# Rows of the expert slots turned by transposing loads from 16-bit planes, and four products of a kind in a row

## The reference

```
xn = layernorm(x)
y  = x + attention(xn) + ffn(xn)

attention: q = xn Wq^T + bq (16 heads of 16), k, v = one shared head of 16 each
           strictly causal softmax(q k^T / 4) v, then Wo, bo
ffn:       scores = sigmoid(xn w_router); 32 experts in 8 groups; 4 groups, then 6 experts are picked per token
           routed = sum over the picked e of score_e * (silu(xn gate_e) * (xn up_e)) down_e      (M = 176)
           shared = (silu(xn sh_gate) * (xn sh_up)) sh_down                                       (352 wide)
```

## Time and profile before

| | us |
|---|---|
| median of 3 runs | 644.38 |
| lowest, highest | 642.62, 650.23 |
| the profiled execution's span | 648.6 |
| PE busy in it | 579.2 (89%) |
| POOL, DVE, ACT busy | 324.4, 350.6, 277.4 |

### The profile page before, as it was taken

How to read it: one execution, slowest core, us unless ns; L and a number is a source line. 1 busy time by engine, 2 the same in 40 slices (tenths; PEclk the granted TensorE clock), 3 DMA queues, 4 the chain that set the end, 5 groups by cost and what they waited for, 6 DMA issues and landing times.

```text
span 648.6 us, 12417 instructions
## 1 busy us (share of the span) xinstructions
PE 579.2 (89%) x4250; PEld 331.8 (51%) x4250; DVE 350.6 (54%) x921; ACT 277.4 (43%) x537; POOL 324.4 (50%) x265
## 2 busy tenths in 40 slices
PE   4998887888999899999799999999999999999900
PEld 2444333444555455464456566665656566565700
DVE  6637684894675566211355555546455554546136
ACT  2755223344543443546445454554545354454200
POOL 5122330320466755775046566666767676767600
PEclk9999998998999899999999999999999999999965
DMA  8697988699699963699346665566565655666598
GB/s 304 182 170 104 376 322 275 47 351 368 191 299 347 362 201 119 191 338 368 123 100 106 114 126 91 96 108 130 88 125 89 121 94 117 110 108 95 63 334 325
DMA packets 72555, 122.84 MB, mean 189 GB/s; under 512 B 10864, under 2 KB 56112, under 8 KB 71984
## 3 DMA queue, kind: packets, MB, share of 16 engines
q1 hardware_dynamic: 47808, 85.02, 43.8%
q0 software_dynamic: 20736, 29.05, 24.2%
q10 hardware_dynamic: 3952, 8.00, 3.5%
HBM read 61.41 MB, written 62.52 MB: 191 GB/s over the span
## 4 chain that ended last, share of the span: by engine, by line
PE 45%; POOL 15%; issue 14%; DMA 13%; DVE 8%; ACT 3%; SPq 1%; ACTq 0%; DVEq 0%; POOLq 0%
POOL acc_d L1319 13%; PE bank L1553 8%; PE bank L1583 5%; DMA acc_d<-attT,xnT 5%; PE bank L1423 5%; PE bank L1405 5%; PE bank L1379 4%; DVE mx L948 3%; PE bank L1494 3%; DMA k_d<-weights 2%; PE bank L1486 2%; PE bank L1352 2%; PE bank L1407 2%; DMA weights<-mpart 2%; PE bank L1382 2%
## 5 line engine op out<-in xcount | busy, mean ns | idle before, releaser
L1319 POOL DMA_INDIRECT acc_d<-attT,xnT x112 | 192.6, 1720 | 122.2 <-DMA acc_d<-attT,xnT 73.6
L1553 PE MATMUL bank<-weights,xnT 128*64 x448 | 143.4, 462 | 1.8 <-DVE attT L1101 1.7
L1276 POOL DMA_INDIRECT xg_d<-stage,posu x96 | 92.5, 963 | 75.4 <-issue 55.1
L948 DVE TENSOR_REDUCE mx<-bank 128x1 f32<-128x384 f32 (+7 forms) x154 | 105.1, 708 | 43.3 <-PE bank L1382 40.9
L766 ACT ACTIVATE xnT<-bank 128x1024 f32<-128x1024 f32 (+1 forms) x72 | 62.0, 884 | 81.0 <-PE bank L1407 76.4
L1553 PEld LDWEIGHTS bank<-weights,xnT 128*64 128x64 f32 x448 | 58.7, 136 | 63.0 <-issue 51.4
L827 ACT ACTIVATE attT<-bank,xnT 128x256 f32<-128x256 f32 x112 | 46.9, 470 | 83.1 <-PE bank L1586 83.1
L1556 PE MATMUL bank<-attT,xnT 128*64 128x352 f32 x224 | 76.9, 466 | 0.0
L1556 PE MATMUL bank<-shared_sb,xnT 128*64 128x352 f32 x224 | 75.5, 459 | 0.0
L812 ACT ACTIVATE xnT<-bank 128x176 f32<-128x176 f32 x112 | 35.5, 317 | 72.9 <-PE bank L1556 72.9
L1101 DVE COPY attT<-weights 128x704 f32 x56 | 29.5, 527 | 48.9 <-PE bank L1556 41.2
(11 more groups left out here) (161 smaller groups left out, 1094.8 us busy)
## 6 DMA issues: line engine op xcount, KB each, us to landing
weights<-in_wts SPq DMA_DIRECT2D x32, 608.0 KB
xg_d<-weights SPq DMA_DIRECT2D x28, 584.0 KB, 9.5
stage<-xg_d SPq DMA_DIRECT2D x14, 584.0 KB, 4.1
xnT<-xg_d SPq DMA_DIRECT2D x14, 584.0 KB
acc_d<-weights SPq DMA_DIRECT2D x8, 512.0 KB, 10.2
q_d<-weights SPq DMA_DIRECT2D x8, 384.0 KB, 5.5
weights<-q_d SPq DMA_DIRECT2D x12, 256.0 KB, 8.8
weights<-q_d SPq DMA_DIRECT2D x48, 64.0 KB, 6.6
```

Of the source, the lines that this page charges most:

```text
L948: eng.tensor_reduce(mx[:, b % 2, h0:h0 + nh * pair, i].rearrange("p (k h) -> p k h", k=pair), bank[:, k:k + pair, 0:wide].rearrange("p k ( ...
L1276: eng.indirect_dma_start(out=xg_d[:, :], out_offset=bass.IndirectOffsetOnAxis(ap=posu[:, t, k:k + 1], axis=0), in_=stage[:, t % NST, :], i ...
L1319: eng.indirect_dma_start(out=acc_d[a][:, :], out_offset=bass.IndirectOffsetOnAxis(ap=index[:, i // RS % NIX, i % RS:i % RS + 1], axis=0), ...
L1553: eng.matmul(bank[0:SR, k, 0:2 * M], rows[:, c, 0:SR], weights[:, bass.ds(expert[i] * WCOL + c * 2 * M, 2 * M)], start=(c == 0), stop=(c = ...
```

## The change

- Rows are kept in DRAM in another form. POOL splits each normalized row of 256 float32 into two planes of 16-bit words (`part_planes`): first the low halves of all columns, then the high halves. Eight copies, two tiles each, into `planes`, which holds four tiles. `rows(g)` stores `planes` in place of `xn`, all eight on SP. `normalize` of tiles 8 to 15 waits for `part_planes` in place of the store.
- The rows of a round come from DRAM by a transposing load (`load_turned`) of 512 rows by 512 16-bit columns into `rows16` (one buffer, in the place of `stage`), and the 36 last words of each row by a load of their own (`load_tails`, two buffers, 144 bytes a row).
- DVE copies the low halves (`merge_low`) and ACT the high halves (`merge_high`) of four slots into `xgT`, each second 16-bit word, which makes float32 of them again. `pair_turn` and `pair_turned` are gone.
- In a round PE does the four gate/up products, then the four down products of the round before. "sb" has the four banks 0 to 3 in place of 2 and 3.
- The views for the slot stage move, so that only columns 1024 to 2047 of `xnT` hold them beside `xgT`.

```diff
+            def load_turned(j):
+                if j == 0:
+                    for n in range(NST):
+                        w.wait_ge(sent[n], 16 * TOPK * NT // NST)
+                for done in merged_half if j else ():
+                    w.wait_ge(done, j)
+                eng.dma_start_transpose(rows16, xg_d16[RS * j * P:RS * (j + 1) * P, 0:2 * D]).then_inc(turned_in, 16)
+
+            def load_tails(j):
+                if j == 1:
+                    k, n = used["down", B - 2, IT - 1]
+                    w.wait_ge(filled[k], n)
+                if j >= 2:
                     w.wait_ge(weight_done, j - 1)
...
-                    load_rows(0)
+                    load_turned(0)
+                    load_tails(0)
+            load_turned(1)
             for j in range(1, ROUNDS):
-                load_rows(j)
+                load_tails(j)
+                if j + 1 < ROUNDS:
+                    load_turned(j + 1)
...
+            def merge_high(j):
+                w.wait_ge(turned_in, 16 * (j + 1))
+                w.wait_ge(pv_done, nth["PV", B - 1, NG - 1, 1])
+                if j >= 2:
+                    k, n = used["sb", RS * (j - 1) - 1]
+                    w.wait_ge(filled[k], n)
+                eng.copy(halves[j % 2][:, :, :, 1], rows16[:, KC:, :]).then_inc(merged_half[1], 1)
...
             for j in range(ROUNDS + 1):
-                for n in range(2):
-                    for i in slots_of(j, n) if j else ():
-                        if i + 2 < NSLOT:
-                            second_gate_up(i + 2)
-                        slot_gated(i)
-                    for i in slots_of(j - 1, 1) if n == 0 else ():
-                        second_down(i)
+                for n, i in enumerate(slots_of(j)) if j else ():
+                    if i + 2 < NSLOT:
+                        second_gate_up(i + 2)
+                    slot_gated(i)
+                    if n == 1 and j + 1 < ROUNDS:
+                        merge_low(j + 1)
+                if j == 0:
+                    merge_low(1)
+                for i in slots_of(j - 1)[2:] if j else ():
+                    second_down(i)
                 if j < ROUNDS:
                     round_weights(j)
-                for i in slots_of(j, 0):
+                for i in slots_of(j)[0:2]:
                     second_down(i)
...
+            def part_planes(g):
+                w.wait_ge(norm_done, 2 * g + 2)
+                if g >= 2:
+                    w.wait_ge(row_out[(g - 2) % 4], 16 * ((g - 2) // 4 + 1))
+                s, s4 = 2 * g % NXN, 2 * g % 4
+                eng.tensor_copy(planes[:, s4:s4 + 2, :].bitcast(U16).rearrange("p t (h d) -> p t h d", h=2),
+                                xn[:, s:s + 2, :].bitcast(U16).rearrange("p t (d h) -> p t h d", h=2)).then_inc(planes_done, 1)
...
-                k2, n2 = used["sa", i // 2]
-                w.wait_ge(emptied[k2], n2)
+                for done in merged_half:
+                    w.wait_ge(done, i // RS + 1)
                 w.wait_ge(second_gu_done, i + 1)
-                rows = xgT[i // 2 % 2][:, i % 2]
+                rows = xgT[i // RS % 2][:, :, i % RS * P:(i % RS + 1) * P]
...
             for j in range(ROUNDS + 1):
-                for n in range(2):
-                    for i in slots_of(j, n) if j else ():
-                        slot_gate_up(i)
-                    for i in slots_of(j - 1, n):
-                        slot_down(i)
-                for p in pairs_of(j + 1):
-                    pair_turn(p)
+                for i in slots_of(j) if j else ():
+                    slot_gate_up(i)
+                for i in slots_of(j - 1):
+                    slot_down(i)
                 for p in pairs_of(j):
                     pair_turn_hidden(p)
```

More of the change, by code:

```diff
@@ L46 @@
 ROW = TOKEN + 4
+TAIL = ROW - D
+PLANES = 2 * D // P
 HUGE = 3e38
@@ L256, in make_plan @@
     steps += attend_steps(streams)
-    steps += [("sa", 0), ("heads", B - 1, NG - 1), ("sa", 1), *[("sb", i) for i in range(RS)],
-              ("attT", B - 1, 0), ("attT", B - 1, 1)]
+    steps += [("begin",), ("heads", B - 1, NG - 1), *[("sb", i) for i in range(RS)], ("attT", B - 1, 0), ("attT", B - 1, 1)]
     plan = Plan()
@@ L364, in build @@
         lrec = sbv("lrec", [P, 2, IT, ST_GROUP])
+        planes = carve([4, D])
         q32 = carve([NPB, T])
@@ L618, in load @@
                     w.wait_ge(comb_out, 16)
+                    for i in range(4):
+                        w.wait_ge(row_out[i], 32)
                     w.wait_ge(init_in, 16 * INITS)
@@ L1081, in round_weights, with merge_low @@
                 own.mark(eng.tensor_tensor(weight[:, j % NIX, :, 0:E], weight[:, j % NIX, :, 0:E],
-                                           xg[j % 2][:, :, D:TOKEN], ALU.mult))
+                                           tails[j % 2][:, :, 0:E], ALU.mult))
                 w.wait_ge(dve_step, own.n)
                 eng.tensor_reduce(weight[:, j % NIX, :, E], weight[:, j % NIX, :, 0:E], AX, ALU.add).then_inc(weight_done, 1)
+            def merge_low(j):
+                w.wait_ge(turned_in, 16 * (j + 1))
+                w.wait_ge(pv_done, nth["PV", B - 1, NG - 1, 1])
+                if j >= 2:
+                    k, n = used["sb", RS * (j - 1) - 1]
+                    w.wait_ge(filled[k], n)
+                eng.tensor_copy(halves[j % 2][:, :, :, 0], rows16[:, 0:KC, :]).then_inc(merged_half[0], 1)
             second = {}
@@ L1163, in vector_program @@
                     with_bias(*a)
-                elif kind == "sa" and a[0] < 2:
-                    second_gate_up(*a)
+                elif kind == "begin":
+                    second_gate_up(0)
+                    merge_low(0)
+                    second_gate_up(1)
                 elif kind == "sb":
@@ L1287, in gpsimd_program @@
                         deviations(*a)
+                elif kind == "rows":
+                    part_planes(*a)
                 elif kind == "proj2" and sub_by[tuple(a)] == "pool":
@@ L1523, in last_down @@
                 ins.then_inc(filled[k], 1)
-            def pair_turn(p):
-                k, n = used["sa", p]
-                for k2, n2 in before["sa", p]:
-                    w.wait_ge(emptied[k2], n2)
-                j = p // 2
-                w.wait_ge(gathered[j % 2], 16 * (j // 2 + 1))
-                for m in range(2):
-                    for c in range(KC):
-                        ins = eng.transpose(bank[:, k, (KC * m + c) * P:(KC * m + c + 1) * P],
-                                            xg[j % 2][:, 2 * p % RS + m, c * P:(c + 1) * P], id_sb)
-                ins.then_inc(filled[k], 1)
             expert = {}
```

126 lines of the change are left out of this document (53 added, 73 removed).

## The result

The kernel after took 661.44 us (median of four runs, 654.69 to 666.49), the kernel before on the same chip 645.11 (642.62 to 650.23): a ratio of 1.019, 95% interval 1.012 to 1.026. (Ratios compare only executions in the faster of two states that the times fall into, so they are not the quotients of the medians, here 1.025.) I had forecast 627. The profiled execution was 660.4 us long by its span, 11.8 more than before. The medians differ by 16.3: the profiled execution of before was the longest of its four (650.23), and where the other 4.5 us lie the profiles don't show.

The account below looks back on a forecast made before the run. PE's rounds (10.24 us) and POOL's add chain (10.49) were taken to bound the kernel. 28 rounds save 20.7 us, early terms add 3.1: 644.4 - 17.6 = 627; own range 612 to 638, reaching 690 for 8 in 10.

Parts of the forecast that it names:

- The planes on POOL: Early part: eight part_planes copies at 1.2 us each, with waits for row stores, add 2 us.
- a rival of 11 us: Early part: planes copies at 2.36 us and slow stores cost 11 us instead of 2, so 636; no chance given.
- My own sign of being wrong: Attention start: prediction is wrong if PE's first row-max matmul comes more than 4 us later than now.
- The start: Start of the slots: PE waits for merge_low(0) between the first two gate-weight copies, +1.1 us.
- The transposing load: Rounds' row load: lands in 6 us, between bounds of 4.1 and 11.2, hidden below about 8 us.
- The merges: DVE's merge_low 1.1 us, its cover just used up (0.1 or 0.2 us); ACT's merge 1.02 us, with room.
- PE's own round: Slot rounds on PE: without the turning matmuls, 0.93 us a round, 10.24 us becomes 9.31.
- The sentence that the order costs nothing: Four gate/up, then four down: same matmuls, may gain a tenth or two, counted as nothing; adds queue but links separate them.
- The round: 28 slot rounds: 10.34 us falls to 9.6, between ends of 9.31 and 10.49, taking 20.7 us off.
- what happens to the add chain: POOL's accumulating stores: two links take 8.48 us without a load, 10.49 with full collision; 1.1 lost, so 9.6.
- the rival that the add chain keeps the pace: Slot rounds: the load hits the odd link squarely, a round of 10.1 to 10.5 us, 641 to 652; chance 0.25.
- The sum: Whole kernel: 20.7 us off in the rounds, 3.1 on early, -17.6 in all, giving 627.

Follow-up runs that it names:

- e1: The kernel after with the last planes split and its store moved behind the second batch's projections: 654.65 us, ratio 1.008.
- e13: The kernel after with the old order (two gate/up, two down, twice) and without transposing loads from round 2 on: 633.35 us, ratio 0.976.
- e2: The kernel after with the transposing loads of rounds 2 and later left out: 647.73 us, ratio 0.998.
- e3: The kernel after with three index buffers in place of two for round_weights: 652.97 us, ratio 1.004.
- e4: The kernel after with three DRAM accumulators in place of two, the third not added to the output: 663.33 us, ratio 1.024.
- e9: The kernel after with the old order again (two gate/up, two down, twice), transposing loads and merges kept: 681.16 us, ratio 1.050.

## Why the prediction was wrong, step by step

- **The planes on POOL, booked at 2 us.** The copies cost what I said (1.08 us each; I took 1.2), and the norms came some 2 us late as said (the last at 28.55 us; 26.54). The step that failed is what queues behind. I listed deviations(6) and (7) and stopped there; behind part_planes(7) on POOL stands split_rest of the second batch, and the store it waits for stands on SP behind the first stack and took 13.7 us, inside the 2.4 to 14.5 of the earlier trace rows. The term was 12.4. I had a rival of 11 us for it, by another mechanism (slow copies, slow stores in front of planes(4)), and gave it no chance of its own; that the sizes agree is luck. e1 shows the mechanism. My own sign of being wrong, first row-max matmul more than 4 us late, came true.
- **The start, booked at 1.1 us.** 2.1: the merge cost 0.5, and 1.5 came from the last expert's load, behind the issue of the transposing load, which holds SP for 2.0 us and which I had at the plain load's 0.4.
- **The transposing load, 6 us to landing.** 5.7: right, and hidden. The Trainium skill's page "VectorE: DVE Perf Modes" (The three transpose paths) gives 1309 ns for a 128 x 128 block by DMA; one after another that was an estimated 21 us for sixteen. The trace does not bear that out for a load of sixteen blocks.
- **The merges.** DVE 0.78 us (I took 1.1), ACT 1.35 (I took 1.02). Neither moved the round: e13 has both and runs at PE's own time.
- **PE's own round, 9.31 us.** Right for the old order (e13, 9.37), mis-sized for the new one (9.55 to 9.65). I took the time of four downs as what was left of 9.31, 3.5 us; it is 3.74. The sentence that the order costs nothing was wrong.
- **The round, 9.6 us, the largest term.** 10.23, so 20.7 us became 2.4. The step that failed is "what happens to the add chain": I took the round as the longer of PE's 9.31 and two links, 8.48 with 1.1 for a part collision, and took 10.49 from the earlier trace rows for the length of the full collision, though two links are a round by definition. The runs show a PE time of 9.55 to 9.65 and, on top, 0.6 to 0.7 us in front of the third product, where PE waits behind round_weights for a landing. The profile of before had shown that path, in the very rows that I quoted: round_weights waits 3.52 us for a landing and PE's products stand behind it. This loop through a landing, DVE, PE, ACT and four adds on POOL opens when the load goes (e2) or a third buffer comes (e3), and not when the accumulators alone are freed (e4). The round lies in the range of the rival that the add chain keeps the pace (10.1 to 10.5), which I gave half the chance of the forecast; that it does is partly luck, since in that rival the links set the pace, and e4 shows that freeing them alone changes nothing. Its time, 641 to 652, was missed by the early part.
- **The sum.** -20.7 + 3.1 was forecast, -2.4 + 14.5 and -0.3 at the end was found: +11.8 in the span. The 4.5 us more by which the medians differ have no term.

## What to carry to other kernels

Where an engine is 99% busy and a chain of transfers is about as long, taking work off the engine gives little until the chain is cut too: look for what waits for the landing, and give it a buffer more, before the work is taken off. Then look at the end: an engine that runs ahead of the adds waits for them there. When a step is put on a queue with a wait on a transfer, follow that queue to the next thing that PE needs, and the transfer to the place on its queue where it is issued. And a transfer's price is also what it does to the transfers that it meets: in the mean the same load cost 0.6 us a round in one order and 1.65 in the other. Look at single rounds before a mean is explained; the longest and the shortest say more.

## What the runs showed of the hardware that I had not expected

- A transposing load of 512 KB of two-byte elements holds SP's queue for 1.3 to 3.7 us per issue in the kernel after (2.04 and 3.57 in the rows above, 2.97 in e9), the plain load of 584 KB for 0.36.
- It makes the packets small. The kernel after has 83,440 packets under 512 bytes, e2, with 26 transposing loads fewer, 29,360: 2,080 for each load of 512 KB. (Before there were 10,864; the 144-byte tails account for 14,336 of the rise.) The DMA share from 380 to 550 us is 0.77 where it had been 0.60, at about the same GB/s (109 and 107). Without the load the share is 0.55, at 63 GB/s (e2).
- An accumulating store on POOL takes 1.56 us in some places of a round and up to 2.18 in others (up to 2.52 in e9). The one that starts right behind round_weights took 2.15 or 2.16 us in the kernels before, after and e9 alike. I did not test the cause.
- A 16-bit copy of 128 x 1024 with a stride of two elements on one side takes 775 ns on DVE and 1348 on ACT, which write with the stride, and 1076 on POOL, which reads with it.
